# Second layer's cross with its context prepared ahead, queries turned before keys, and halves of the outputs apart

## What is computed

```
x = x + _L1_attn_ref(_layernorm(x), ...)                       # latent attention
x = x + _L1_xattn_ref(ctx, _layernorm(x), mask, ...)
x = x + _L1_ffn_ref(_layernorm(x), ...)
x = x + _L2_attn_ref(_layernorm(x), ...)
x = x + _L2_xattn_ref(_layernorm(x), ctx, ...)
x = x + _L2_ffn_ref(_layernorm(x), ...)
```

```
xn = layernorm(x, ln_x_g, ln_x_b)          # x is the context here
ln = layernorm(latents, ln_l_g, ln_l_b)    # latents is the normed x of the model
q = ln @ Wq.T
kv = jnp.concatenate([xn @ Wkv.T, ln @ Wlkv.T], axis=1)
k, v = (kv[..., :INNER], kv[..., INNER:])
qn = rmsnorm(q, qn_g) * SCALE
kn = rmsnorm(k, kn_g)
attn = jnp.einsum('bhid,bhjd->bhij', qn, kn)
attn = jax.nn.softmax(jnp.where(full_mask, attn, -max), axis=-1)
out = jnp.einsum('bhij,bhjd->bhid', attn, v)
return out @ Wo.T + bo
```

## Time and profile before

| what | us |
|---|---|
| median of 3 runs | 1432.03 |
| the runs | 1428.06 to 1438.11 |
| profiled execution | 1430.51 |
| its span, first to last instruction | 1428.7 |
| PE busy | 1333.0 (93%) |
| DVE busy | 929.2 (65%) |
| ACT busy | 671.9 (47%) |
| POOL busy | 345.4 (24%) |
| mean granted clock of PE, full speed = 1 | 0.979 |

### The profile page before, as it was taken

The page is one execution under the profiler, slowest core; times in us unless marked ns, Lnnn a source line. Parts: engine busy times, 40 slices in busy tenths (PEclk is TensorE's granted clock), DMA queues, the critical chain, the costliest instruction groups (busy, mean ns, idle before and its releaser), DMA issues.

```text
span 1428.7 us, 29436 instructions
## 1 busy us (share of the span) xinstructions
PE 1333.0 (93%) x11626; PEld 861.1 (60%) x11626; DVE 929.2 (65%) x1890; ACT 671.9 (47%) x1697; POOL 345.4 (24%) x373
## 2 busy tenths in 40 slices
PE   8998999999999889999989898899999999999986
PEld 6766565446666765667868586754435555654434
DVE  6776765343667555356684367588888876678755
ACT  5886533342787454344303245425557777740002
POOL 4000330001011100114203011177787465300001
PEclk9999999999999999999999989999999999999998
DMA  3000105100000000000124002101020110699980
GB/s 135 3 2 3 40 0 202 52 29 16 2 2 3 18 1 0 21 4 2 46 99 134 12 7 82 31 16 45 30 59 16 22 26 16 142 220 253 248 198 15
DMA packets 25352, 80.60 MB, mean 56 GB/s; under 512 B 5243, under 2 KB 7306, under 8 KB 24834
## 3 DMA queue, kind: packets, MB, share of 16 engines
q1 hardware_dynamic: 24354, 75.60, 19.4%
q10 hardware_dynamic: 864, 3.15, 0.8%
HBM read 72.17 MB, written 1.08 MB: 51 GB/s over the span
## 4 chain that ended last, share of the span: by engine, by line
PE 75%; DVE 11%; ACT 5%; DMA 4%; issue 3%; POOL 1%; SPq 0%; DVEq 0%; ACTq 0%; POOLq 0%
PE psum L2967 7%; PE psum L196 7%; PE psum L431 5%; PE psum L2988 5%; PE psum L2681 4%; PE psum L1267 4%; PE psum L2637 4%; PE psum L1261 3%; PE psum L451 3%; PE psum L2651 3%; PE psum L495 2%; PE psum L674 2%; DMA heads<-scratch_out_gates 2%; PE psum L2690 2%; DMA context_v<-scratch_out_gates 2%
## 5 line engine op out<-in xcount | busy, mean ns | idle before, releaser
L196 PE MATMUL psum<-ident 128*128 128x128 f32 x1272 | 159.6, 284 | 9.1 <-DMA ident<-in_ident 3.8
L187 POOL TENSOR_TENSOR rstd<-var,minus_half 128x4 f32<-128x4 f32 x30 | 31.3, 1043 | 557.9 <-DVE var L144 528.4
L196 PEld LDWEIGHTS psum<-ident 128*128 128x128 f32 x1272 | 153.2, 199 | 17.1 <-issue 7.7
L574 DVE TENSOR_REDUCE quad_max<-psum 128x1 f32<-128x128 f32 (+3 forms) x256 | 113.1, 484 | 55.8 <-PE psum L435 53.9
L529 ACT ACTIVATE pt<-psum,quad_max 128x128 f32<-128x128 f32 (+3 forms) x256 | 133.3, 530 | 26.7 <-DVE quad_max L574 26.6
L2988 PE MATMUL psum<-pt,slots 128*128 128x512 f32 x256 | 114.6, 599 | 5.0 <-DVE pt L3142 4.7
L2967 PE MATMUL psum<-slots,xn_t 128*128 128x512 f32 x256 | 113.9, 605 | 3.1 <-DVEq L3113 3.1
L2726 ACT ACTIVATE p<-psum,duo_max 128x512 f32<-128x512 f32 x128 | 86.8, 683 | 41.8 <-DVE duo_max L2761 41.7
L3057 ACT ACTIVATE pt<-psum,p 128x64 f32<-128x64 f32 x256 | 57.8, 392 | 72.7 <-POOL wide L3199 41.9
L2988 PEld LDWEIGHTS psum<-pt,slots 128*128 128x128 f32 x256 | 47.1, 189 | 71.7 <-issue 48.8
L2967 PEld LDWEIGHTS psum<-slots,xn_t 128*128 128x128 f32 x256 | 49.6, 194 | 66.0 <-issue 57.8
(11 more groups left out here) (515 smaller groups left out, 2796.8 us busy)
## 6 DMA issues: line engine op xcount, KB each, us to landing
pt<-scratch_out_gates SPq DMA_DIRECT2D x32, 256.0 KB, 12.9
heads<-scratch_out_gates SPq DMA_DIRECT2D x24, 256.0 KB, 15.6
slots<-in_s_l0f SPq DMA_DIRECT2D x8, 514.0 KB, 3.3
wide<-scratch_gates SPq DMA_DIRECT2D x8, 512.0 KB, 6.9
slots<-in_s_l3v SPq DMA_DIRECT2D x8, 512.0 KB, 3.7
context_v<-scratch_out_gates SPq DMA_DIRECT2D x16, 256.0 KB, 18.1
slots<-in_s_l3o ACTq DMA_DIRECT2D x6, 512.0 KB, 10.3
weights<-in_w_l1a SPq DMA_DIRECT2D x1, 2624.0 KB, 9.7
```

Source lines behind the costliest of these rows:

```text
L196: nc.tensor.matmul(m.ps[bank][:, 0:P], m.ident[:, :], m.ident[:, :], start=True, stop=True, skip_group_check=True)
L574: nc.vector.tensor_reduce(m.quad_max[:, n % 2, g:g + 1], m.ps[g][:, 0:keys], AX.X, ALU.max, negate=True).then_inc(m.quad_negmax, 1)
```

## The change

1. The context's norm moves from l1x into l1a: statistics, POOL's root and the scaling right behind l1a's own norm (`norm_context`), gain and bias in the middle of l1a's loop (`weight_context`). POOL's root stands ahead of the zeroing of `pair_k`.
2. In l1x PE turns and projects the context ahead of the stage's norm, with 8, 7, 7+2+8 products of `keep_busy` around it instead of 6+13+8 further on (14 of them stand next to each other). DVE squares the context's keys ahead of those of q. ACT copies v behind the square root. PE waits for q, for k and for the context apart. ACT copies the keys' first 64 rows, DVE the second 64. The output of the first sequence is copied, and its half of the projection made, before the second sequence's product with the values.
3. The output projections of l0a, l1a, l1x, l2a and l3x go half by half: x, projection, x, projection.
4. In the loops of l2x and l3x the row sums move from step k for k-5 to step k for k-6, and DVE's division goes one step later.
5. In l2x's tail `x_tensor` takes the place of the last 7 `keep_busy`.
6. In l2f the norm's gain goes into two of ACT's copies as a scale, and DVE uses the plain norm.

```diff
-    x_tensor(nc, pe, m, "l0y")
-    pe.wait_ge(m.quad_scaled, B)
-    tokens_tensor(nc, pe, m, "l0y", m.o_t, w["wo"], on_x=True)
+    for j in range(2):
+        x_tensor(nc, pe, m, "l0y", (j,))
+        pe.wait_ge(m.quad_scaled, j + 1)
+        tokens_tensor(nc, pe, m, "l0y", m.o_t, w["wo"], on_x=True, halves=(j,))
...
+def project_out_half(nc, pe, m, source, name, w, j):
+
+
+    x_tensor(nc, pe, m, name, (j,))
+    copied(m, pe, f"{source}{j}")
+    tokens_tensor(nc, pe, m, name, m.o_t, w, on_x=True, halves=(j,))
...
-                                    for r in range(GROUP)], on_x=True)
+    for j in range(2):
+        x_tensor(nc, pe, m, "l1az", (j,))
+        pe.wait_ge(m.quad_scaled, B + (j + 1) * GROUP)
+        sums_tensor(nc, pe, m, "l1az", [(lambda t, r=r: m.wide[:, r, t * P:(t + 1) * P], m.lat_out[:, r * P:(r + 1) * P])
+                                        for r in range(GROUP)], on_x=True, halves=(j,))
...
+    w, d = m.w["l1x"], m.dve
...
+    each = lambda row: row[0:SC, :].rearrange("p (o d) -> p o d", o=1).broadcast_to([SC, B, DC])
+    d.done(nc.vector.tensor_tensor(m.context[:, :, :], m.context[:, :, :], each(w["ln_x_g"]), ALU.mult))
+    nc.vector.tensor_tensor(m.context[:, :, :], m.context[:, :, :], each(w["ln_x_b"]), ALU.add).then_inc(m.context_normed, 1)
+    nc.vector.tensor_copy(m.low_row[0:1, :], m.mask_low[0:1, B * SC:2 * B * SC]).then_inc(m.low_row_ready, 1)
...
+    dve.wait_ge(m.xn_ready, m.turns_dve)
+    norm_context(nc, dve, m)
...
-    quad_vector(nc, dve, m, a, invert, before={1: take_latents})
+    quad_vector(nc, dve, m, a, invert, before={1: take_latents, SETS // 2: lambda dve: weight_context(nc, dve, m)})
...
     norm_gpsimd(nc, pool, m)
+    m.norms_pool += 2
+    pool.wait_ge(m.var_ready, m.norms_pool)
+    nc.gpsimd.tensor_tensor(m.rstd[0:SC, 0:B], m.var[0:SC, 0:B], m.minus_half[0:SC, 0:B], ALU.pow).then_inc(m.rstd_ready, 2)
     nc.gpsimd.memset(m.pair_k[:, :, :, :], 0.0).then_inc(m.turned_zero, 1)
...
-    busy_through_norm(nc, pe, m, 6, 13, 8)
+    pe.wait_ge(m.context_normed, 1)
+    for b in range(B):
+        last = nc.tensor.transpose(m.ps[4][0:DC, b * SC:(b + 1) * SC], m.context[:, b, :], m.ident[0:SC, 0:SC])
+    last.then_inc(m.ahead_made, 1)
+    keep_busy(nc, m, 8)
+    pe.wait_ge(m.ahead_taken, AHEAD["l1x"] + 1)
+    for b in range(B):
+        nc.tensor.matmul(m.ps[5 - b][0:SC, 0:2 * P], m.context_norm_t[0:DC, b * SC:(b + 1) * SC], w["wkv"][0:DC, :], start=True,
+                         stop=True).then_inc(m.ahead_made, 1)
+    busy_through_norm(nc, pe, m, 7, 2, 8)
     turn_tensor(nc, pe, m, "l1xn")
     turned(nc, m, pe, "l1xn")
     tokens_tensor(nc, pe, m, "l1xq", m.xn_t, w["wq"])
     tokens_tensor(nc, pe, m, "l1xk", m.xn_t, w["wlk"])
     tokens_tensor(nc, pe, m, "l1xv", m.xn_t, w["wlv"])
-    pe.wait_ge(m.context_normed, 1)
...
-    keep_busy(nc, m, 20)
+    keep_busy(nc, m, 16)
     pe.wait_ge(m.rms_done, 1)
-    for name, src in (("l1xqt", m.q_tok), ("l1xkt", m.k_tok)):
+    for n, (name, src) in enumerate((("l1xqt", m.q_tok), ("l1xkt", m.k_tok))):
+        pe.wait_ge(m.rms_done, n + 1)
         for j in range(2):
             bank = fill(m, pe, f"{name}{j}")
             for t in range(4):
                 last = nc.tensor.transpose(bank[:, t * P:(t + 1) * P], src[:, 4 * j + t, :], m.ident[:, :])
-            last.then_inc(filled(m, f"{name}{j}"), 1)
+            last.then_inc(filled(m, f"{name}{j}"), n + 1)
+    pe.wait_ge(m.rms_done, 3)
     bank = fill(m, pe, "l1xct0")
     for b in range(B):
         last = nc.tensor.transpose(bank[:, b * SC:(b + 1) * SC], m.context_kv[0:SC, b, 0:P], m.ident[0:SC, 0:SC])
-    last.then_inc(filled(m, "l1xct0"), 1)
+    last.then_inc(filled(m, "l1xct0"), 2)
     for name in ("l1xqt0", "l1xqt1", "l1xkt0", "l1xkt1", "l1xct0"):
-        copied(m, pe, name)
+        copied(m, pe, name, 0 if "q" in name else 1)
...
         if j >= 0 and (j + 1) % (2 * NQ) == 0:
             b = j // (2 * NQ)
+            if b == 1:
+                project_out_half(nc, pe, m, "l1xo", "l1xy", w["wo"], 0)
...
-    project_out_tensor(nc, pe, m, "l1xo", "l1xy", w["wo"])
+    project_out_half(nc, pe, m, "l1xo", "l1xy", w["wo"], 1)
...
-    take_x(nc, act, m, "l1az", 6)
+    act.wait_ge(m.ahead_made, AHEAD["l1x"] + 1)
+    nc.scalar.activation(m.context_norm_t[0:DC, :], m.ps[4][0:DC, 0:B * SC], ACT.Copy).then_inc(m.ahead_taken, 1)
+    take_x(nc, act, m, "l1az", 7)
+    for b in range(B):
+        act.wait_ge(m.ahead_made, AHEAD["l1x"] + 2 + b)
+        nc.scalar.activation(m.context_kv[0:SC, b, :], m.ps[5 - b][0:SC, 0:2 * P], ACT.Copy).then_inc(m.ahead_taken, 1)
...
+    def take(name, dst):
         for j in range(2):
             bank = read(m, act, f"{name}{j}")
             nc.scalar.activation(dst[:, 4 * j:4 * j + 4, :], bank[:, :].rearrange("p (t d) -> p t d", d=P),
                                  ACT.Copy).then_inc(emptied(m, f"{name}{j}"), 1)
...
+    take("l1xq", m.q_tok)
+    take("l1xk", m.k_tok)
     act.wait_ge(m.rms_ready, 1)
     nc.scalar.activation(m.rms[:, :], m.rms[:, :], ACT.Sqrt).then_inc(m.rms_inverted, 1)
+    take("l1xv", m.v)
...
+    first = slice(0, 64)
     for j in range(2):
         bank = read(m, act, f"l1xkt{j}")
-        for h in range(2):
-            own = slice(64 * h, 64 * h + 64)
-            last = nc.scalar.activation(m.pair_k[own, 0, h, j * S:(j + 1) * S], bank[own, :], ACT.Copy,
-                                        scale=w["kn_g"][own, :])
-        last.then_inc(emptied(m, f"l1xkt{j}"), 1)
+        nc.scalar.activation(m.pair_k[first, 0, 0, j * S:(j + 1) * S], bank[first, :], ACT.Copy,
+                             scale=w["kn_g"][first, :]).then_inc(emptied(m, f"l1xkt{j}"), 1)
     bank = read(m, act, "l1xct0")
-    for h in range(2):
-        own = slice(64 * h, 64 * h + 64)
-        last = nc.scalar.activation(m.pair_k[own, 1, h, 0:B * SC], bank[own, 0:B * SC], ACT.Copy, scale=w["kn_g"][own, :])
-    last.then_inc(emptied(m, "l1xct0"), 1)
+    nc.scalar.activation(m.pair_k[first, 1, 0, 0:B * SC], bank[first, 0:B * SC], ACT.Copy,
+                         scale=w["kn_g"][first, :]).then_inc(emptied(m, "l1xct0"), 1)
...
-    copy_out_scalar(nc, act, m, "l1xo", m.o_t)
+        if k in (2 * NQ + 5, XSTEPS + 1):
+            b = 0 if k < XSTEPS else 1
+            bank = read(m, act, f"l1xo{b}")
+            nc.scalar.activation(m.o_t[:, b * S:(b + 1) * S], bank[:, :], ACT.Copy).then_inc(emptied(m, f"l1xo{b}"), 1)
...
+    dve.wait_ge(m.ahead_taken, AHEAD["l1x"] + 3)
+    ck = m.context_kv[0:SC, :, 0:P]
+    d.done(nc.vector.tensor_tensor(m.squares[0:SC, 0:B, :], ck, ck, ALU.mult))
+    d.done(nc.vector.tensor_reduce(m.rms[0:SC, 4 * NT:4 * NT + 2 * B], heads(m.squares[0:SC, 0:B, :]), AX.X, ALU.add))
     for name, src, at in (("l1xq", m.q_tok, 0), ("l1xk", m.k_tok, 2 * NT)):
         for j in range(2):
             copied(m, dve, f"{name}{j}")
...
     nc.vector.reciprocal(m.rms[:, :], m.rms[:, :]).then_inc(m.rms_ready, 1)
     dve.wait_ge(m.rms_inverted, 1)
     q_r = m.rms[:, 0:2 * NT]
     d.done(nc.vector.tensor_scalar(q_r, q_r, float(64 ** -0.5), None, ALU.mult))
     spread = lambda ap, n: ap.rearrange("p (t o) -> p t o", o=1).broadcast_to([ap.shape[0], n, 64])
-    nc.vector.tensor_tensor(heads(m.q_tok), heads(m.q_tok), spread(q_r, 2 * NT), ALU.mult)
-    nc.vector.tensor_tensor(heads(m.k_tok), heads(m.k_tok), spread(m.rms[:, 2 * NT:4 * NT], 2 * NT), ALU.mult)
+    nc.vector.tensor_tensor(heads(m.q_tok), heads(m.q_tok), spread(q_r, 2 * NT), ALU.mult).then_inc(m.rms_done, 1)
+    nc.vector.tensor_tensor(heads(m.k_tok), heads(m.k_tok), spread(m.rms[:, 2 * NT:4 * NT], 2 * NT), ALU.mult).then_inc(
+        m.rms_done, 1)
     ckh = ck.rearrange("p b (h d) -> p b h d", d=64)
...
-
+    second = slice(64, P)
+    dve.wait_ge(m.turned_zero, 1)
+    for j in range(2):
+        bank = read(m, dve, f"l1xkt{j}")
+        nc.vector.tensor_scalar(m.pair_k[second, 0, 1, j * S:(j + 1) * S], bank[second, :], w["kn_g"][second, :], None,
+                                ALU.mult).then_inc(emptied(m, f"l1xkt{j}"), 1)
+    bank = read(m, dve, "l1xct0")
+    nc.vector.tensor_scalar(m.pair_k[second, 1, 1, 0:B * SC], bank[second, 0:B * SC], w["kn_g"][second, :], None,
+                            ALU.mult).then_inc(emptied(m, "l1xct0"), 1)
...
-    project_out_tensor(nc, pe, m, "l2ao", "l2ay", w["wo"])
+    for j in range(2):
+        project_out_half(nc, pe, m, "l2ao", "l2ay", w["wo"], j)
...
-        n = k - 6
+        n = k - 7
...
+            n = k - 6
+            if n >= 0 and n % 2 == 1:
+                b, _, qt = units[n]
+                name = f"{stage}o{n // 2}"
+                bank = m.ps[m.items[name][0]]
...
             bank = fill(m, pe, f"{stage}h0")
             nc.tensor.matmul(bank[:, 0:1], m.ones_row[0:1, :], m.number[0:1, 1:2], start=True,
                              stop=True).then_inc(filled(m, f"{stage}h0"), 1)
-            keep_busy(nc, m, 7, 0)
```

(19 more changed lines are left out.)

104 lines of the change are left out of this document (34 added, 70 removed).

## The result

| what | before | after |
|---|---|---|
| median | 1432.31 us (4 runs) | 1414.27 us (4 runs, 1410.10 to 1418.27) |
| profiled execution | 1430.51 us | 1410.10 us |
| span | 1428.7 us | 1408.3 us |
| mean granted clock | 0.979 | 0.989 |

The ratio of the times is 0.9875, with a 95% interval of 0.9845 to 0.9905. Timed again beside the last experiments it was 0.9869 (0.9829 to 0.9908), with five executions of the changed kernel from 1403.67 to 1418.48 us; a sixth took 7247 us and is left out as disturbed. The median of 1414.27 lies 0.5 us under the forecast of 1414.8. Faster by 1.25% is what was called likeliest. Not all of it is the change's: both kernels run at two levels of TensorE's clock, and the changed one's executions had more of the full one, as the account of the prediction shows.

What follows compares the result with a forecast made beforehand. PE was taken to hold 75% of the chain of waits, with gains only where it idles or runs fill products. Terms summed to -17.25 us: profiled 1430.5 to 1413.3, median 1414.8, range 1407 to 1425.

Steps and rivals of the forecast that it cites:

- The cross's front: Second layer's cross, ahead of its scores: earlier q scaling, q turned first and key copies on two engines bring scores 4.2 us earlier.
- about 4 us nearer: Sign of being right: the second layer's cross scores start about 4 us nearer to q's scaling.
- The clock there: At the second layer's cross scores: the clock falls to half speed again, so the 3.1 us lost there stay lost.
- Rival 2: The clock does not fall in front of the second layer's scores: -3.1 us, total 1411.7; chance 0.15.
- The latent attention: l1a: zeroing behind the context's root no longer delays xn, -0.3 us; output projection by halves, -0.1.
- rival 3: Latent attention: POOL's zeroing locks out DVE where it matters, price up to 3.5 us, total 1418.3; chance 0.07.
- Halves: Output projections by halves: -0.7 us in l0a, -0.5 in l2a, -1.3 in l3x, -0.3 in l1x.
- The third layer's loop: Third layer's cross loop: with the row sums moved, pairs of steps take 5.11 us instead of 5.59, -4.5 over five.
- the bound for a repeated stretch: Third layer's cross loop: if only the spell of half clock repeats, the gain is -2.1 us instead of -4.5.
- Its tail: Third layer's cross tail: x's turn into PSUM takes the place of `keep_busy`, -1.7 us, between -1.8 and 0.
- The fourth layer's loop: Fourth layer's cross loop: pairs drop from 5.11 us to PE's own 4.48, -3.9 us, between 0 and -4.6.
- l2f: Norm's gain as a scale in ACT's copies: 0.09 us more on each of four copies, +0.25 us.

## Why the prediction was right

By its own steps:

- **The cross's front, -4.2.** Right by its steps. The way to the turn grew by 0.37 us (5.95 from the last projection of the stage before, against 5.58), where 0.45 was said; from the turn to the scores it is 16.76 against 21.30, so -4.54 where -4.65 was said. From q's scaling to the scores it is 3.16 nearer; the sign "about 4 us nearer" was too high by the forecast's own sums, which have 3.3. Undoing the split and the order singly gave 1.8 and about 1.0.
- **The clock there.** I took it that it falls again, and in the profiled execution it did; that step was right by luck. Over the eight traces with the same stretch it falls in five, for 3.4 or 6.8 us, and in three not at all. The reason given (little busy there) is at most a part of it, as the same stretch was followed by full clock in three traces. Rival 2 is no rival but a share of the executions.
- **The latent attention, -0.3 and -0.1.** Together -0.67 (the turn to the last projection: before from 347.41 to 493.48, after from 346.12 to 491.52), but not by the step named. The turn of xn and the eight products behind it took 3.01 us before and 2.36 after, and half speed lasted until about 349.4 in the one trace and 346.9 in the other (granted clock 0.64 in 348 to 350, 0.78 in 346 to 348). By those clocks I estimate 0.6 of the 0.65 as the clock's. In the trace before it was a weight load that waited 0.3 us for xn while PE shows no gap, and with the zeroing put first again nothing waited, so that the 0.3 as a gain is not shown; that the sum fits is luck. The zeroing started at 345.30, 2 us sooner than I had it, as xn was through sooner, and the context's scaling was locked out for all of it. That is rival 3's mechanism, which I gave 0.07 as an event and which came at no price: it ended 1.5 us before DVE was needed. The Trainium skill, SBUF — State Buffer, Who interferes with whom, says that of DVE in its two-port mode and GpSimd whoever issues first keeps the other out for its whole instruction. The traces agree: POOL was first both times (345.30 against 345.39, and with the zeroing put first 344.90 against 344.98), and one DVE operation stood for 3.5 us.
- **Halves: -0.7, -0.5, -1.3, -0.3.** -0.66, -0.57, and in the fourth layer's cross 10.50 against 9.37 us from x to the next turn, -1.13, since PE still waits 0.33 us for POOL. In the second layer's cross it was nothing (-0.03): PE waits 0.70 us for ACT's copy of the second half there, which the forecast's -0.3 did not count, though it named such a wait as a sign of being wrong.
- **The third layer's loop, -4.5.** 5.16 a pair where 5.11 was said, 24.87 us for five pairs where 25.55 was said, and no half-speed stretch. With the lags put back it was 27.48, so the change itself is worth 2.6, where the bound for a repeated stretch said -2.1 (5 x (5.59 - 5.11) of its own pairs would be 2.4), and the other 2.6 is the stretch of the execution before. The forecast named the sum; which part is the change's only the experiment tells. Pairs of 5.11 with 4.48 of PE's work can't be without a bracket on the turns, as the signs had it: they wait 0.23 and 0.55, and the clips wait 0.32 and 0.64, which was a sign of being wrong and was none.
- **Its tail, -1.7.** -1.38: the return comes 0.25 us later than the turn of x could start.
- **The fourth layer's loop, -3.9.** -3.54: 3.15 in the five pairs, to the hundredth but by two misses that cancel (4.54 in four of them where 4.48 was said, 4.24 in the fifth), and 0.39 instead of 0.75 at the end.
- **l2f, +0.25.** +0.86 in these two traces, which had their half-speed stretches at different places. Three traces of the experiments with the same one stretch as before (lags back, more fill, the changed kernel again) took 104.12 to 104.13 us, against 103.92: +0.2.

The sum of the touched stages is -17.2 against -17.5, of which about 3 (the loop's stretch and the latent attention) is clock. The profiled execution came out at 1410.1, not 1413.3, for it had fewer half-speed stretches elsewhere.

That the median fits to 0.5 us is luck in part. The record has nineteen executions of the kernel before beside the experiments, at a mean granted clock of 0.972 to 0.983 (0.978 on average), and nine of the changed one at 0.977 to 0.991 (0.985). In both kernels an execution is about 1.0 us longer for each 0.001 of clock less. By a line fitted to these 28 executions I estimate the change at 12.7 us for equal clock, give or take 2.3, and the other 7 of the 19.7 us between the two averages went with the higher clock. The forecast had counted on little of that. Whether the change brings the higher clock or these executions happened to have it, no run here decides.

## What to carry to other kernels

Walk the longest way round a loop through all engines, with two steps if even and odd differ, and look on it for an instruction that waits in its queue behind one that it doesn't need: swapping a copy and an exponential was worth as much (2.5 us) as moving the row sums and the division (2.6). Products that only keep the clock up are a fixed bill in front of a wait; when the work that they cover gets shorter, count them anew: here cutting them brought the turns forward by 9.5 us without a loss in the mean clock. But compare from turn to turn behind the cut too, since one stage gave all of its 1.1 us back in a wait and another had a longer half-speed stretch. And when a program's own executions differ by 1%, compare intervals between landmarks, and hold totals against the granted clock before you give them to the change.

## What the runs showed of the hardware

I had taken the granted clock's falls as an effect of what the kernel does at a place. Over thirteen traces of nearly one program they come at the same few places (335 to 355 us and 705 to 740 us in all of them), at others by chance: near 240 us in seven of thirteen, near 515 us for 0, 3.4 or 6.8 us behind the same 2.53 busy of 5.00 us. The mean clock of executions of the changed kernel went from 0.977 to 0.991, and their times from 1418 to 1404 us with it. Eight transposes in float32 ran in 1.06 us at a granted clock of 1.00. The stage that streams gates was the second source: 470.8 to 481.3 us between the same turns.
